# Fetching gathered attention rows by indirect DMA and DMA transposes in place of one-hot matmuls

## What is computed

```
h = tok(x)                        # embedding row, RMS norm, projection, RMS norm: depends on the token alone
q, k = feature_map(ln(h) Wq), feature_map(ln(h) Wk); v = ln(h) Wv      # 16 heads of 32
attn = tril(einsum('bqhd,bkhd->bhqk', q / sqrt(32), k) ** 2)
h = h + (attn v / (sum attn + eps)) Wo
h = h + W_down(hadamard(silu(x_gate) * x_up)),  x_gate, x_up = hadamard(ln(h)) W_gate, W_up    # 512 -> 2048 -> 512
```

## Time and profile before

| | us |
|---|---|
| median of 3 runs (range) | 1403.45 (1400.7 to 1405.17) |
| the profiled execution's own time | 1400.2 |
| its span, first to last instruction | 1398.4 |
| PE busy | 1306.7 (93%) |
| DVE busy | 532.3 (38%) |
| POOL busy | 422.9 (30%) |
| ACT busy | 398.7 (29%) |

### The profile page before, as it was taken

The page is one execution under the profiler, slowest core; times in us unless marked ns, Lnnn a source line. Parts: engine busy times, 40 slices in busy tenths (PEclk is TensorE's granted clock), DMA queues, the critical chain, the costliest instruction groups (busy, mean ns, idle before and its releaser), DMA issues.

```text
span 1398.4 us, 19203 instructions
## 1 busy us (share of the span) xinstructions
PE 1306.7 (93%) x7481; PEld 643.6 (46%) x7481; DVE 532.3 (38%) x1049; ACT 398.7 (29%) x703; POOL 422.9 (30%) x371
## 2 busy tenths in 40 slices
PE   5575598989999999999999999999999999999999
PEld 3352255554444444444444444444444444444444
DVE  1655567654422253226222432234222523251110
ACT  4453463440233113321233023311322123211220
POOL 0342143332144313432244213421433124321210
PEclk9888699999999999999999999999999999999999
DMA  8911100002100130003000210012001300020000
GB/s 297 288 27 23 24 1 9 8 8 54 53 8 9 31 75 8 15 15 80 19 16 8 68 38 8 15 42 64 8 8 23 83 8 15 15 68 23 0 0 30
DMA packets 101681, 55.73 MB, mean 40 GB/s; under 512 B 74180, under 2 KB 90872, under 8 KB 101112
## 3 DMA queue, kind: packets, MB, share of 16 engines
q1 hardware_dynamic: 98112, 45.77, 12.8%
q0 software_dynamic: 2560, 8.39, 2.0%
q10 hardware_dynamic: 952, 0.75, 0.2%
HBM read 29.47 MB, written 8.65 MB: 27 GB/s over the span
## 4 chain that ended last, share of the span: by engine, by line
PE 83%; DVE 6%; DMA 4%; ACT 4%; issue 2%; POOL 1%; SPq 0%; DVEq 0%; ACTq 0%
PE bank L1078 24%; PE bank L1079 24%; PE bank L1080 23%; DMA prod<-sg 3%; PE bank L1231 3%; PE bank L1073 2%; PE bank L1216 2%; PE bank L1215 2%; PE bank L1121 1%; DMA hid<-in_L_tok_norm_weight 1%; PE bank L1240 1%; ACT xT L855 1%; DVE wgu L477 1%; PE bank L1071 1%; ACT wgu L855 1%
## 5 line engine op out<-in xcount | busy, mean ns | idle before, releaser
L1078 PE MATMUL bank<-xT,wgu 128*128 128x512 f16 x1024 | 389.3, 380 | 1.4 <-DVE xT L708 1.4
L1079 PE MATMUL bank<-xT,wgu 128*128 128x512 f16 x1024 | 389.3, 380 | 0.0
L1080 PE MATMUL bank<-xT,wgu 128*128 128x512 f16 x1024 | 389.2, 380 | 0.0
L398 POOL TENSOR_TENSOR hid<-a,hid 128x512 f16<-128x512 f32 x128 | 147.9, 1156 | 512.0 <-ACT hid L855 512.0
L743 DVE SCALAR_TENSOR_TENSOR a<-bank,kap,sg 128x512 f32<-128x512 f32 x128 | 96.0, 750 | 477.5 <-PE bank L1080 324.4
L1078 PE MATMUL bank<-wd,hid 128*128 128x512 f16 x512 | 194.3, 379 | 0.0
L1079 PE MATMUL bank<-wd,hid 128*128 128x512 f16 x512 | 194.1, 379 | 0.0
L1080 PE MATMUL bank<-wd,hid 128*128 128x512 f16 x512 | 194.0, 379 | 0.0
L358 POOL TENSOR_TENSOR p<-prod,p 128x512 f16<-128x512 f32 x128 | 153.2, 1199 | 128.4 <-ACT p L855 128.4
L855 ACT ACTIVATE hid<-a 128x512 f16<-128x512 f32 x128 | 80.6, 630 | 279.5 <-DVE a L743 279.5
L1080 PEld LDWEIGHTS bank<-xT,wgu 128*128 128x128 f16 x1024 | 100.4, 98 | 121.6 <-issue 1.4
(11 more groups left out here) (178 smaller groups left out, 1245.8 us busy)
## 6 DMA issues: line engine op xcount, KB each, us to landing
out<-a SPq DMA_DIRECT2D x24, 256.0 KB, 2.2
wgu<-in_L_ffn_W_gate SPq DMA_DIRECT2D x16, 256.0 KB, 5.5
wgu<-in_L_ffn_W_up SPq DMA_DIRECT2D x16, 256.0 KB, 5.0
wd<-in_L_ffn_W_down SPq DMA_DIRECT2D x4, 1024.0 KB, 9.4
ids_b<-in_x SPq DMA_DIRECT2D x8, 256.0 KB, 3.5
out<-h_row SPq DMA_DIRECT2D x8, 256.0 KB, 2.0
xT<-in_L_tok_proj_weight SPq DMA_DIRECT2D x1, 1024.0 KB, 8.6
p<-in_L_attn_Wq SPq DMA_DIRECT2D x1, 1024.0 KB, 13.8
```

The lines of the kernel that those rows point to most:

```text
L398: nc.gpsimd.tensor_tensor(hid[:, 1, s, :], a32[:, :], hid[:, 0, s, :], ALU.subtract)\
L1078: mm(dst, w[0], v[0], start=first, stop=False)
L1079: mm(dst, w[0], v[1], start=False, stop=False)
L1080: return mm(dst, w[1], v[0], start=False, stop=final)
```

## The change

Block 0 stays as it is. For blocks 1 to 7 PE no longer picks. The score table is stored once to DRAM as four tables `att_table0` to `att_table3` (four heads, high and low halves: 1024 fp16 values per token). For each quad of heads and each 128 positions (`m` = 0 to 3), POOL issues an indirect DMA that fetches 128 rows of 2 KB (`gather`, L422) into a staging buffer, and SP issues a DMA transpose of 128x1024 (`p_turn`, L296) from it into the quad's buffer of high and low halves. There are two staging buffers ("ways"): for quads 1 to 3, m = 0 and 2 use the first and m = 1 and 3 the second; quad 0 uses only the first. A gather waits until the transpose before it from the same staging buffer has landed, and a transpose waits for its gather. The second staging buffer lies in `hid`, the first in `ids_b`. The quads' buffers are two, `p16` and one in the place of `att`.

The gathers of quads 1, 2 and 3 are issued in slots 0 to 11, one per slot, after POOL's product and feed subtractions; those of quad 0 of the block after, in slots 12, 14, 18 and 25. DVE adds the fetched high and low halves into `prod` (L763), then multiplies in place by `cnt` (L768); it waits at heads 0, 4, 8 and 12 for the quad's transposes. ACT no longer waits for `heads_ready` before its copy to `p16`. POOL's loop over blocks is written out instead of a `Fori`.

```diff
+NEXT_AT = (12, 14, 18, 25)
...
+def fetched(n, q, m):
+    if q == 0:
+        return 0, 10 * (n - 1) + m
+    if m % 2 == 0:
+        return 0, 10 * (n - 1) + 4 + 2 * (q - 1) + m // 2
+    return 1, 6 * (n - 1) + 2 * (q - 1) + m // 2
...
+        p_even = att[:, :, :, :].rearrange("p l h v -> p (l h v)").rearrange("p (l j t) -> p l j t", l=2, j=4)
+        PB = [p_even, p16]
+        stages = [ids_b[:, :].bitcast(F16), hid[:, 0, FT - 2:FT, :].rearrange("p a b -> p (a b)")]
...
+            def store_tables():
+                sp.wait_ge(S["a_lo"], 4)
+                for q in range(QUADS):
+                    nc.sync.dma_start(att_tables[q].rearrange("t (l h v) -> t l h v", l=2, v=P),
+                                      att[:, :, 4 * q:4 * q + 4, :]).then_inc(S["tab_stored"], 16)
...
+            def p_turn(n, q, m):
+                way, g = fetched(n, q, m)
+                sp.wait_ge(S[f"pg_land{way}"], 16 * g + 16)
+                if n == 1 and q == 0 and m == 0:
+                    sp.wait_ge(S["tab_stored"], 64)
+                    sp.wait_ge(S["picked"], H)
+                if m == 0 and (n, q) != (1, 0):
+                    sp.wait_ge(S["heads_ready"], QUADS * n + q - 1)
+                nc.sync.dma_start_transpose(PB[q % 2][:, :, :, m * P:(m + 1) * P].rearrange("p l j t -> p (l j) t"),
+                                            stages[way]).then_inc(S[f"pt_land{way}"], 16)
...
                 for q in range(QUADS):
                     if turning is not None:
+                        for m in range(4):
+                            if q < 3:
+                                p_turn(turning, q + 1, m)
+                            elif turning < NB - 1 and m < 2:
+                                p_turn(turning + 1, 0, m)
+                        if q == 2 and turning < NB - 1:
+                            load_gather_ids(turning + 1)
                         o_turn(turning, q)
+                if turning is not None and turning < NB - 1:
+                    p_turn(turning + 1, 0, 2)
...
+            def gather(n, q, m):
+                way, g = fetched(n, q, m)
...
+                if not (first(n - 1) and m == way and q == way):
+                    pool.wait_ge(S[f"pt_land{way}"], 16 * g)
+                nc.gpsimd.indirect_dma_start(stages[way], None, att_tables[q],
+                                             bass.IndirectOffsetOnAxis(ids_p[:, m:m + 1].bitcast(U32), axis=0))\
+                    .then_inc(S[f"pg_land{way}"], 16)
+
+            def fetch(n, s):
+                if s < H - 4:
+                    gather(n, s // 4 + 1, s % 4)
+                elif s in NEXT_AT and not (isinstance(n, int) and n == NB - 1):
+                    gather(n + 1, 0, NEXT_AT.index(s))
...
                 feed(b, s)
                 if s == 0:
                     product(b + 1, s)
+                fetch(b + 1, s)
                 attend(b + 1, s)
...
-                    nc.vector.tensor_tensor(prod[:, s % 2, :], PICK[s % 2][:, :], cnt[:, :], ALU.mult)\
-                        .then_inc(S["p_done"], 1)
+                    else:
+                        raw = PB[s // 4 % 2]
+                        if s % 4 == 0:
+                            for way in range(2 if s else 1):
+                                dve.wait_ge(S[f"pt_land{way}"], 16 * fetched(n, s // 4, 2 + way if s else 3)[1] + 16)
...
+                        nc.vector.tensor_tensor(prod[:, s % 2, :], raw[:, 0, s % 4, :], raw[:, 1, s % 4, :], ALU.add)\
+                            .then_inc(S["ps_done"], 1)
...
+                        nc.vector.tensor_tensor(prod[:, s % 2, :], prod[:, s % 2, :], cnt[:, :], ALU.mult)\
+                            .then_inc(S["p_done"], 1)
...
-                for h in (0, 1) if s == 0 else (s + 1,) if s + 1 < H else ():
-                    i = H * n + h
+                for h in () if not zero else (0, 1) if s == 0 else (s + 1,) if s + 1 < H else ():
```

More of the change, by code:

```diff
@@ L293, in block_io @@
                 for m in range(4):
-                    if n is not None and m == 2:
-                        load_ids_rows(n)
+                    if m == 3 and turning is not None and turning < NB - 1:
+                        p_turn(turning + 1, 0, 3)
                     if n is not None and m == 3:
@@ L306, in block_io @@
                         x_turn(turning, m + 1)
-            load_ids_rows(1)
+            load_gather_ids(1)
+            store_tables()
             for q in range(QUADS):
+                if q == 3:
+                    for m in range(2):
+                        p_turn(1, 0, m)
                 o_turn(0, q)
+            p_turn(1, 0, 2)
             for m in range(4):
+                if m == 3:
+                    p_turn(1, 0, 3)
                 x_turn(0, m)
@@ L402, in _ @@
                 product(0, s)
+                if s in NEXT_AT:
+                    gather(1, 0, NEXT_AT.index(s))
                 attend(0, s)
@@ L419, in _ @@
                 product(1, s)
+                fetch(1, s)
                 attend(1, s)
@@ L426, in _ @@
                     bound_power(2)
-            with pool.Fori(1, NB - 1) as b:
+            for b in range(1, NB - 1):
                 for s in range(SLOTS):
@@ L996, in feed_high @@
                 if s < FT:
+                    if s == FT - 2 and not (isinstance(b, int) and b == NB - 1):
+                        act.wait_ge(S["pt_land1"], 96 * (b + 1))
                     act.wait_ge(S["a_done"], FT * b + s + 1)
@@ L1195, in attend @@
             def attend(n, s):
+                zero = isinstance(n, int) and n == 0
+                tokens = onehot0 if zero else onehot
                 if s == 0:
```

75 lines of the change are left out of this document (49 added, 26 removed).

## The result

| | us |
|---|---|
| after, median of 4 runs (range) | 1488.98 (1487.0 to 1490.35) |
| before, median of 4 runs (range), same chip | 1404.31 (1400.7 to 1405.55) |
| ratio, 95% interval | 1.0615 (1.0595 to 1.0636) |
| the profiled execution's own time / its span | 1490.35 / 1488.5 |

The kernel became 6.15% slower. The forecast was 1479, the range 1418 to 1525.

A forecast was written before the change was run, and what follows sets the result against it. PE was taken to bound the loop, busy 874.76 of 880 us. The profiled 1400.2 us plus 59 (loop), 15 (block 0's feed) and 2 (attention) gave 1476; the median, 3.25 above the profiled execution, 1479, range 1418 to 1525.

The forecast's parts named there:

- Picks leave PE: In each loop block PE loses 16 pick pairs of 0.43 us: a gain of 6.9 us per block.
- Four waits per block, at slots 6, 10, 14 and 15: PE's loop waits: three for DVE's a(s), one for POOL's product at slot 15, 14.8 us per block.
- First quad, wait of 1.6: Slot 6 of a loop block: PE waits 1.6 us for a(4), behind the late fetch chain.
- Quads 2 and 3, 4.4 each: Later quads of a loop block: fetch chain 1.6, POOL's backlog 0.4 and collisions 2.4, so 4.4 us each.
- Slot 15, 4.4: PE waits for the low half of head 15 behind the same POOL backlog: 4.4 us per block.
- Clock, +2 (0 to 4.8): In the loop, PE's granted clock drops after long waits: 2 us per block, bounds 0 and 4.8.
- Loop in all: Blocks 2 to 7, the loop's six rounds: +9.9 us per block, +59 in all.
- Feed of block 0, +15, and attention, +2: Ahead of the loop: block 0's feed beside block 1 +15 us (+4 to +25), its attention +2 (0 to 5).
- No collisions, 1415: Rival: DVE and POOL do not collide, waits of 7.3 us offset the picks per block; 1415 us, chance 0.13.
- Longer legs: Rival: each gather and transpose takes 1 us more under load, loop 48 us longer; 1533 us, chance 0.12.
- The DMA engines' load: In the loop, 20 to 24 more transfers of 256 KB per block keep the DMA engines below half, from 13%.
- The hidden chain, 1365: Rival: turned rows arrive early enough that PE never waits in the loop, picks are a gain; 1365 us, chance 0.05.

The follow-up runs named there:

- e8: The changed kernel without gathers and transposes (DVE adds constants instead), with PE's loop over blocks 1 to 6 written out: 1354.3 us, 142.7 per block.
- e2: The changed kernel with DVE's two product instructions each reading one SBUF and one PSUM operand (low half of the score left out): 1463.9 us.
- e4: The changed kernel without gathers and transposes of fetched rows; DVE adds two stretches of a constant SBUF tile instead: 1364.9 us.
- e10: The changed kernel with gathers in pairs, counts from PSUM, quad 0 fetched later, feed first in slots 4, 8, 12, PE's loop written out: 1368.1 us.

## Why the prediction was right, point by point

The forecast of 1479 was 10 us (0.7%) under the median, slower was right, and the mechanism stood: fetch chain, then collisions, then clock. That it came so near is in part luck, since errors cancel. The block of the loop (mean of the five from 396.12 to 1203.72) closes as follows: e8's 142.7 with none of these waits; plus 9.4 of waits for `a(s)` and 2.5 for head 15; plus 1.4 of pause, which the first round does not have; plus 5.1 of clock: 161.1, against 161.5 measured. The forecast had 14.8 of waits (11.9 measured), 2 of clock (5.1) and no pause (1.4).

- *Picks leave PE*, forecast 6.9 us per block: 149.8 - 142.7 = 7.1. Right.
- *Four waits per block, at slots 6, 10, 14 and 15*: 18 and 6 in six blocks. Right in number and in what ends them. DVE's wait ahead of its add, which was to be 3 to 6 us, was 9.6 in the mean; the forecast's own chain gives 8.7 (rows turned at U + 9.5, `a(3)` made by U + 0.8), so that sign did not follow from it.
- *First quad, wait of 1.6*: 1.62 in a quad of e2, 2.65 in one of the change. The term that was too small is the gather: 3.4 us by the earlier trace rows, 4.63 from its issue to that of its transpose, where the transpose of the other staging buffer was on its way.
- *Quads 2 and 3, 4.4 each*: the three waits of one block were 2.65, 4.33 and 2.89, their sum 9.9 against the forecast's 10.4. POOL's backlog was worked out as 0.6 for ACT, 13.0 of work and 2.4 of collisions, from `a(4)`'s end to that of slot 7's subtraction: 16.0. It was 15.5 (754.49 to 769.95). The 2.4 were placed wrongly in part: POOL's own subtractions there were stretched by only 0.5 us, and the rest came as idle time of POOL behind three stretched instructions of DVE (1.8 us in all).
- *Slot 15, 4.4*: 2.5. Too large; I had taken the backlog of quads 2 and 3, with a gather in each slot, and there only two of four slots have one.
- *Clock, +2 (0 to 4.8)*: 5.1, outside its bounds. The step that failed is "but a slower PE shortens the wait after it", by which three drops of 1.6 us became 2 us in all. In the block from 716 to 880 us there were four, each of 1.7 us, after the pause of 2.01 and the waits of 4.33, 2.89 and 2.21; the wait of 2.65 had none. So the drops came at more waits than the forecast counted.
- *The pause at the loop's start*: not in the forecast, 1.7 us in a round that has it, 1.4 per block in the mean. The forecast had taken PE's loop as the old one less its picks; e8 shows that its new body costs something at the jump.
- *Loop in all*: +9.9 forecast, +11.3 over six rounds.
- *Feed of block 0, +15, and attention, +2*: first `a(s)` at 177.30 instead of 171.65, so 5.7 for the attention, outside its bounds of 0 to 5, and 16.9 for the feed. By e4 all of it is the fetch: without it DVE's load and the missing picks together made -0.6, where the forecast had 5.6 - 6.9 = -1.3. Pairs take 13.3 of the 22.6 away. `x_turn` 3 did stand behind a transpose of fetched rows (161.65 and then 162.97 on SP, 157.16 before), but was 5.8 us later and not 0.6: the mechanism was right and this term mis-sized. From the first matmul the attention is 7.5 us longer.
- *No collisions, 1415*: this rival was tried as e2, which had none and took 1464. Its four waits of 7.3 us were 8.9, with a pause of 1.6 and 3.7 us of clock beside them: it had left out the wait for the staging buffer, the pause, and the clock that goes with them.
- *Longer legs*: half true. In the loop the medians were 3.6 and 3.1, near the rows, but single transposes took up to 5.1. And the gathers into the second staging buffer, which fetch the last rows of a quad, took 4.1 in the median of the whole program, 0.7 over the row:

```profile
hid<-att_table,ids_p POOLq DMA_INDIRECT x42, 4.1
```

- *The DMA engines' load*: the forecast counted 20 to 24 transfers more per block; the change adds 16 gathers and 16 transposes. Their share was 0.35 in the loop, still below half.
- *The hidden chain, 1365*: e10 is this rival made true by other edits, 1368.

The Trainium skill's rule in "SBUF — State Buffer", section "Who interferes with whom", held for the 128x512 pairs: a DVE instruction with one SBUF operand never stretched (e2), one with two did (e4). In e2 the two instructions took 674 to 690 ns in all cases, in e4 up to 830 and 1177. What such stretches are worth the runs show: no wait of PE in e4, none for `a(s)` or a head in e10, and 4.5 us per block in the change, where DVE and POOL were late already.

## What to carry to other kernels

A wait in an in-order queue is priced by what stands behind it, and that is two prices: how late the waited-for thing is, and how far the queue must run to catch up. Moving the wait behind one instruction did little here (2.7 us per block, beside 11.9 of waits), because the fetch was late by more than what was moved ahead of it; with the fetch issued earlier as well, and the other edits of e10, no such wait was left. Before counting the gain of work that leaves the bounding engine, list what the remaining work waits for: here 7.1 us per block were given up by PE and 18.9 were put on the path.
